# Weights asked for a step sooner, empty rows written in three parts, and first row numbers noted ahead of the scales, in an expert layer

## The reference

```python
x = conv_attention(x)      # group norm, 1x1 qkv, softmax attention, 1x1 out, + normed x
t = to_tokens(x)           # 4 x 1024 tokens of 256
t = t + attention(layernorm(t))          # three residual MLPs, softmax over axis 1, Wout
y = layernorm(layernorm(t)) # with gain and bias the second time
p = softmax(y @ gate_w); keep = top2(p)
out = sum over experts e of keep[:, e] * (gelu(y @ w1[e] + b1[e]) @ w2[e] + b2[e])
t = t + layernorm(t) + out
```

## Time and profile before

| what | us |
|---|---|
| median of 3 runs (lowest, highest) | 1253.4 (1251.55, 1254.43) |
| the profiled execution | 1251.13 |
| its span in the trace | 1249.4 |
| PE busy | 1150.2 (92%) |
| DVE busy | 815.4 (65%) |
| ACT busy | 572.1 (46%) |
| POOL busy | 255.2 (20%) |
| first to last turn mark of the weighted steps, X(2) to X(26) | 359.0 for 24 steps |
| X(26) to X(36) | 116.6 for 10 steps, none with new weights |

### The profile page before, as it was taken

How to read it: one execution, slowest core, us unless ns; L and a number is a source line. 1 busy time by engine, 2 the same in 40 slices (tenths; PEclk the granted TensorE clock), 3 DMA queues, 4 the chain that set the end, 5 groups by cost and what they waited for, 6 DMA issues and landing times.

```text
span 1249.4 us, 24976 instructions
## 1 busy us (share of the span) xinstructions
PE 1150.2 (92%) x8066; PEld 1068.1 (85%) x8067; DVE 815.4 (65%) x1931; ACT 572.1 (46%) x1042; POOL 255.2 (20%) x307
## 2 busy tenths in 40 slices
PE   6999999999999999999999879869789888899993
PEld 5898998988988989989888869869789888899983
DVE  4676476765666855767646777866777788756641
ACT  2433344432536333444324556645556556534431
POOL 2010001000401001411005122344223222323320
PEclk9999999999999999999999989979899999999996
DMA  5001000100101100101003352676674676433238
GB/s 165 1 1 34 1 1 1 35 34 1 63 12 35 34 1 14 59 1 34 1 1 135 99 166 55 187 208 183 193 218 128 182 214 200 116 55 61 57 52 274
DMA packets 82436, 103.50 MB, mean 83 GB/s; under 512 B 11952, under 2 KB 71600, under 8 KB 82352
## 3 DMA queue, kind: packets, MB, share of 16 engines
q1 hardware_dynamic: 68912, 85.10, 21.3%
q0 software_dynamic: 13440, 17.32, 7.4%
HBM read 74.19 MB, written 29.25 MB: 83 GB/s over the span
## 4 chain that ended last, share of the span: by engine, by line
PE 67%; DMA 10%; issue 7%; DVE 6%; SPq 4%; ACT 2%; POOL 2%; POOLq 1%; another core or an unknown queue 0%; ACTq 0%; DVEq 0%
PE ps L1659 59%; DMA w1r<-in_w 4%; DMA acc_rows<-y_w,now_s 4%; PE ps L1753 2%; PE ps L1672 1%; SPq L539 1%; PE ps L1701 1%; DVE w1s L1524 1%; DMA rows<-acc_rows 1%; DVE hs L1622 1%; PE ps L1924 1%; DVE hs L1624 1%; PE ps L1762 1%; PE ps L1775 1%; DVE tl_bn L1144 1%
## 5 line engine op out<-in xcount | busy, mean ns | idle before, releaser
L1659 PE MATMUL ps<-w2s,hs 128*128 128x256 f32 x1728 | 258.1, 285 | 53.0 <-DVE hs L1624 52.8
L1659 PEld LDWEIGHTS ps<-w2s,hs 128*128 128x128 f32 x1728 | 227.0, 193 | 61.3 <-DVE hs L1624 50.4
L1659 PE MATMUL ps<-xt,w1s 128*128 128x256 f32 x1746 | 260.4, 286 | 1.0 <-issue 1.0
L1659 PEld LDWEIGHTS ps<-xt,w1s 128*128 128x128 f32 x1746 | 229.3, 192 | 1.8 <-issue 1.6
L1013 ACT ACTIVATE h<-ps,b1t 128x256 f32<-128x256 f32 x288 | 137.5, 478 | 103.6 <-PE ps L1659 60.0
L750 POOL DMA_INDIRECT acc_rows<-y_w,now_s x72 | 120.3, 1670 | 185.7 <-ACT y_w L1031 120.2
L1624 DVE TENSOR_TENSOR hs<-h,hs 128x256 fp32r<-128x256 f32 x288 | 123.6, 429 | 9.9
L1622 DVE CAST hs<-h 128x256 fp32r<-128x256 f32 x288 | 89.1, 309 | 58.3 <-ACT h L1013 33.9
L1659 PE MATMUL ps<-xs,wh 128*128 128x512 f32 x384 | 121.4, 397 | 1.4 <-issue 1.4
L1659 PEld LDWEIGHTS ps<-vk,pr 128*128 128x128 f32 x768 | 95.8, 190 | 5.1 <-DVE pr L1478 3.0
L1659 PE MATMUL ps<-vk,pr 128*128 128x256 f32 x768 | 97.2, 282 | 2.1 <-DVE pr L1478 2.1
(11 more groups left out here) (232 smaller groups left out, 1779.1 us busy)
## 6 DMA issues: line engine op xcount, KB each, us to landing
w1r<-in_w SPq DMA_DIRECT2D x22, 1024.0 KB
w2r<-in_w SPq DMA_DIRECT2D x22, 1024.0 KB, 8.4
xg<-sorted_rows SPq DMA_DIRECT2D x38, 272.0 KB
b2t<-in_b SPq DMA_DIRECT2D x37, 128.0 KB
xn<-in_x SPq DMA_DIRECT2D x4, 1024.0 KB, 4.8
acc_rows<-r_out SPq DMA_DIRECT2D x4, 1024.0 KB
rows<-acc_rows SPq DMA_DIRECT2D x8, 512.0 KB, 7.7
out_tokens<-cols_out SPq DMA_DIRECT2D x8, 512.0 KB, 8.6
```

The costliest lines, as they stand in the source:

```text
L1659: ins = t.matmul(out, left[l], right[r], start=first and n == 0, stop=last and n == 2, **more)
```

## The change

1. SP's order in turn s becomes `load_weights(s+2)`, `gather(s+2)`, `load_biases(s+1)`, and turn 0 has the weights too. `load_weights(s+2)` waits until the weights of step s are split, where `load_weights(s+1)` waited for those of step s - 1.
2. `write_pads` is cut in three: two blocks at turn 6, three at 7, four at 9.
3. POOL notes steps 0 and 1 before the two `tail_scales`. For this `now_s` and `now_w` get a place of their own.
4. One more pair (steps 10 and 11) is written out, since turn 10 now loads weights of step 12. The waits for the second table (`tab_b`) move along with it.
5. In step 0 PE turns the next rows in chunk 2 and no longer in chunk 1.

```diff
-    LOOP_AT = A_STEPS // 2 - 1
+    LOOP_AT = A_STEPS // 2
...
+        PADS_AT = {6: (0, 1), 7: (2, 3, 4), 9: (5, 6, 7, 8)}
+        ROWS_OUT_AT = 8
...
             def steps(i):                                   # SP
                 for n in range(2):
                     s = i * 2 + n
-                    begin = isinstance(i, int) and s == 0
-                    if not begin:
-                        load_weights(s + 1, 1 - n, (i if n == 0 else i + 1))
+                    unrolled = isinstance(i, int)
+                    if unrolled and s == A_STEPS - 2:
+                        sp.wait_ge(tab_b, 1)
+                    load_weights(s + 2, n, i + 1)
+                    if unrolled and s == A_STEPS - 2:
+                        sp.wait_ge(pad_in, (E + 1) * 16)
+                        sp.wait_ge(rows_in, B * NT * 2 * 16)
                     gather(s + 2, n, False)
-                    if not begin:
+                    if not (unrolled and s == 0):
                         load_biases(s + 1, 1 - n)
-                    if isinstance(i, int):
-                        if s == 6:
-                            write_pads()
-                        if s == 8:
+                    if unrolled:
+                        if s in PADS_AT:
+                            write_pads(PADS_AT[s])
+                        if s == ROWS_OUT_AT:
                             rows_of(B - 1)
...
-            sp.wait_ge(pad_in, (E + 1) * 16)
-            sp.wait_ge(rows_in, B * NT * 2 * 16)
...
-                    note_step(s + 1, 1 - n, (i if n == 0 else i + 1))
+                    if not (isinstance(i, int) and s == 0):
+                        note_step(s + 1, 1 - n, (i if n == 0 else i + 1))
...
+            pool.wait_ge(tab_a, 1)
+            note_step(0, 0, 0)
+            note_step(1, 1, 0)
             tail_scales(B - 1, 0)
             tail_scales(B - 1, 1)
...
-            pool.wait_ge(tab_a, 1)
-            note_step(0, 0, 0)
             pool.wait_ge(tok_out, B * 16)
...
-                    if f == 1:
+                    if f == (2 if isinstance(i, int) and s == 0 else 1):
                         x_turn(s + 1, 1 - n, (i if n == 0 else i + 1))
```

More of the change, by code:

```diff
@@ L144, in hybrid_block_kernel @@
         last_step = sb("last_step", [P, 1], I32)
-        sb("to_512", [P, 0x10])
+        now_s = sb("now_s", [P, 2, SUB], I32)
+        now_f = sb("now_f", [P, 2 * SUB + 1])
+        now_w = now_f[:, 0:2 * SUB].rearrange("p (n h) -> p n h", n=2)
+        limit = now_f[:, 2 * SUB:2 * SUB + 1]
         batch_scope = ExitStack()
@@ L252, in hybrid_block_kernel @@
         y_b = es("y_b", [P, SUB, C])
-        now_s = es("now_s", [P, 2, SUB], I32)
-        now_w = es("now_w", [P, 2, SUB])
+        es("past_y", [P, 16])
         es("past_prob", [P, 512 - 16 + 64])
@@ L569, in steps, with write_pads @@
                     s = i * 2 + n
-                    begin = isinstance(i, int) and s == 0
-                    if not begin:
-                        load_weights(s + 1, 1 - n, (i if n == 0 else i + 1))
+                    unrolled = isinstance(i, int)
[5 more added lines that the diff above has]
+                        sp.wait_ge(rows_in, B * NT * 2 * 16)
                     gather(s + 2, n, False)
-                    if not begin:
+                    if not (unrolled and s == 0):
                         load_biases(s + 1, 1 - n)
-                    if isinstance(i, int):
-                        if s == 6:
-                            write_pads()
-                        if s == 8:
+                    if unrolled:
+                        if s in PADS_AT:
+                            write_pads(PADS_AT[s])
+                        if s == ROWS_OUT_AT:
                             rows_of(B - 1)
-            def write_pads():
+            def write_pads(experts):
                 sp.wait_ge(tab_b, 1)
                 sp.wait_ge(pad_made, 2)
-                for e in range(E + 1):
+                for e in experts:
                     at_row = sp.value_load(pad_at[0:1, e:e + 1], min_val=0, max_val=PAD - STEP) if e < E else PAD
@@ L768, in _ @@
             g.memset(pad_row[:, NUMBER:NUMBER + 1], float(SKIP)).then_inc(pad_made, 1)
-            pool.wait_ge(tab_a, 1)
-            note_step(0, 0, 0)
             pool.wait_ge(tok_out, B * 16)
             for i in range(LOOP_AT):
+                if i == LOOP_AT - 1:
+                    pool.wait_ge(tab_b, 1)
                 steps(i)
-            pool.wait_ge(tab_b, 1)
             pool.wait_ge(tok_out, (B + 1) * 16)
@@ L1636, in _ @@
             for i in range(LOOP_AT):
+                if i == LOOP_AT - 1:
+                    dve.wait_ge(tab_b, 1)
                 steps(i)
-            dve.wait_ge(tab_b, 1)
             with dve.Fori(LOOP_AT, PAIRS) as i:
```

## The result

The changed kernel took **1209.2 us** (median of four runs, 1206.3 to 1212.2) against 1252.5 us for the one before on the same chip: ratio 0.9653, 95% interval 0.9622 to 0.9684, 43 us less. Forecast were 1212.4 us in a range of 1200 to 1235. The profiled run took 1207.3 us, its span 1205.6, at a clock of 0.991.

What follows compares the result with a forecast made beforehand. The prediction took PE's products (59% of the chain) as the bound wherever PE is fed, with waits for weights above that floor. 1251.1 - 7.6 - 14 - 19.4 = 1210.1, plus 2.3 gives 1212.4 us; range 1200 to 1235.

Steps and rivals of the forecast that it cites:

- Step 1: Early notes and weights ahead of the gather remove DVE's whole wait in step 1: -7.6 us, bounds 5.0 and 9.8.
- Steps 7 to 10: Weights ahead of the empty rows end the 14.26 us wait; POOL's rounds are late next: -14 us, between 9 and 24.7.
- Steps 11 to 14 and 16 to 24: The 13 steps with new weights take 12.6 us each, 163.8 for 183.2: -19.4 us, between -31.6 and -4.5.
- a loop of two steps: In weighted steps: splits done, weights issued and landed, rows and biases, gelu, splits; 24.7 us, or 12.35 a step.
- DVE's own 11.7 a step: In the weighted steps, DVE's pieces and a chunk of splits alone would take 11.0 + 0.7 = 11.7 us.
- A: Biases queue behind weights; with landings of 11.8 us weighted steps take 13.75 to 14.0, the whole 1230 us; chance 0.15.
- C: Late biases or rows make PE stand and its clock fall in weighted steps, 16.0 us each: 1263 us; chance 0.05.
- D: Weights don't go out sooner, since splits end hardly before the note; empty rows and notes alone help: 1240 us; chance 0.05.
- B: Landings shrink, all weighted steps reach PE's floor of 11.66 us, steps 7 to 10 win 20: 1194 us; chance 0.10.
- At nothing: Terms of zero: the written-out pair, moved table waits, places of now_s and now_w, steps 2 to 6, 15, 25 to 35.
- What would show it: Signs: ACT's w1r wait under 15 us, step 1 about 14, step 7 below 16, 13 weighted steps at 12 to 13.

Runs made afterwards that it cites:

- experiment 6: The changed kernel with DVE's low parts made half as wide from step 2 on, the other half stale: 1201.6 us, ratio 0.9583.
- experiment 1: The changed kernel with only the weights a step sooner, all nine blocks of empty rows at turn 6, first notes behind the tail scales: 1206.2 us, ratio 0.9612.
- 4: The changed kernel with the first two notes behind the tail scales again: 1207.0 us, ratio 0.9617.
- experiments 5 to 12: Eight follow-up kernels with edits to weight bytes, DVE's work, SP's order, empty rows or row scatters against the changed kernel: medians 1201.6 to 1213.0 us.
- number 12: The changed kernel with only the row scatters spread over steps 5 to 9 as 1, 2, 2, 2, 1 tiles: 1209.9 us, ratio 0.9673.
- 5: The changed kernel with half the bytes in each transfer of weights from step 2 on, so products use stale weights: 1204.1 us, ratio 0.9615.
- 7: The changed kernel with w2 asked for last, behind rows and biases, so only 1 MB lies ahead of the biases: 1212.6 us, ratio 0.9688.
- 11: The changed kernel with empty rows all at turn 6, notes behind the scales, biases before the gather and row scatters spread: 1205.9 us, ratio 0.9632.
- experiments 1 to 4: Four follow-up kernels that take parts of the change back, against the changed kernel: medians 1206.2 to 1242.3 us.
- 9: The changed kernel with SP issuing the biases of the step ahead before the gather: 1205.8 us, ratio 0.9648.
- 10: The changed kernel with empty rows all at turn 6, notes behind the scales and biases before the gather: 1206.8 us, ratio 0.9648.

## Why the prediction was right

**Step 1: right in size, half right in cause.** -7.65 against -7.6. DVE was what is late next, as the prediction put it: it is busy 15.65 of the 15.9 us, and with its low parts half as wide (experiment 6) step 1 takes 14.2. But the wait did not go because of the notes: experiments 1 and 4 have steps 0 and 1 as short with the notes where they were. That the gather no longer stands ahead of the weights is enough; the prediction gave both reasons and took them for one.

**Steps 7 to 10: right in size, and by luck in part.** Forecast were POOL's notes 7 to 10 in 46 us and 11 from there to X(12). The notes after:

```profile
816.92 0.37 POOL L747 CAST now_s<-xg 128x2 int32<-128x2 f32 x1 [6.51 <-DMA acc_rows<-y_w,now_s]
...
832.53 0.21 POOL L747 CAST now_s<-xg 128x2 int32<-128x2 f32 x1 [3.01 <-DMA acc_rows<-y_w,now_s]
...
847.79 0.32 POOL L747 CAST now_s<-xg 128x2 int32<-128x2 f32 x1 [5.57 <-DMA acc_rows<-y_w,now_s]
...
860.93 0.24 POOL L747 CAST now_s<-xg 128x2 int32<-128x2 f32 x1 [3.48 <-DMA acc_rows<-y_w,now_s]
```

15.6, 15.3 and 13.1 us, 44.0 in all (53.5 in the earlier trace rows's run), and 13.3 from there to X(12); since X(8) now lies 1.3 us ahead of note 7, the gain is 9.5 + 4.5 - 1.3 = 12.7. POOL's rounds came as worked out. But the prediction has gelus wait behind these notes, and in this profile they hardly do: the chain over steps 7 to 10 has no piece of POOL in it, and a fifth of it is `issue` (the view cuts the line off):

```profile
by line: PE ps L1670 32.3%; issue 20.5%; DMA b2t<-in_b 9.4%; another core or an unknown queue 4.5%; DVE w1s L1534 4.5%; DVE hs L1632 4.3%; DVE w2s L1534 3.0%; SPq L519 2.9%; DVEq L1605 2.7%; DVE hs L1634 2.5%; ACT w2s L962 2.1%; SPq L552 1.
```

ACT stands 14.4 us there with nothing named that it waits for, and 3.9 for `b2t`, which waited in SP's queue behind weights that stood for DVE's splits. In experiments 5 to 12, where ACT has no such stands, the mechanism of the prediction shows: landings of the token scatters are 24 to 66% of the chain over these steps (40% in number 12), part of which depends on where the window ends. So the rounds hold this stretch in the runs beside it, and in the profiled run of the change another delay of about the same length stood in their place. That less work on POOL would shorten the stretch is not shown: no run takes any away.

**Steps 11 to 14 and 16 to 24: the size was near, the step of the argument was wrong.** 158.7 us against 163.8, 12.2 a step against 12.6. The prediction closed a loop of two steps over the landing of the weights and the biases behind them and got 24.7 us for it (its 1.5 us for 400 KB at 251 GB/s is 1.6). That two steps took 24.3 is luck: no gelu of the loop waits for biases. Experiments 5 and 7 halve what lies ahead of the biases and leave the pace as it is; experiment 6 eases DVE alone and the pace falls to the floor in eight of nine steps. The term that should have been taken was the one that it named and put aside: DVE's own 11.7 a step (11.60 measured), and in place of the 0.25 for short waits the 1.1 us that each end of a pair costs, half of it a step: 11.62 + 0.55 = 12.17. What exactly happens at the end of a pair (the loop's branch, the two low parts that follow the last chunk, or the first gelu that waits for PE's product) was not separated; that less work on DVE removes it is shown. In the ninth step, 16, late biases cost 3.0 us, by POOL's note and not by weights ahead of them. ACT's waits for `b2t` came to 8.2 us, 3 of them, none in the loop.

**The rivals.** A would have shown in over 25 us of waits for `b2t`: 8.2. C wanted the clock below 0.95 from step 16 on: it is 1.00. D wanted ACT's waits for `w1r`: none is left. B was nearest: the loop lies 0.55 us a step above its floor, and the whole at 1209, between its 1194 and the forecast.

**At nothing**: steps 2 to 6 cost 1.0 us more, since one gelu waits for biases that are issued behind the early weights; step 15 costs 0.8 us more, for which no cause was followed up. The gelu:

```profile
813.24 0.47 ACT L1023 ACTIVATE h<-ps,b1t 128x256 f32<-128x256 f32 x1 [3.45 <-DMA b2t<-in_b]
```

**What would show it**: step 7 was to fall below 16 us and took 17.3 (11.6 to 13.2 in experiments 5 to 12); step 1 was to take about 14 and took 16.0, with step 0 shorter by what it is longer: in experiment 1 the two take 15.8 and 14.1 us, and PE waits 1.98 us for `xg` at X(2), which here it doesn't.

## What to carry to other kernels

Put the transfer with the most slack and the longest landing ahead of those that wait for something in the same queue; here that order is worth 48 us in experiment 1, and 30 us where notes and pads had taken their part already; the finer edits around it add nothing that can be told. Where several loops have about the same length, taking one wait away only shows the next: after a gain, measure each part by itself before keeping it, and ease the supposed bound by half before trusting a sum in which it wins by 5%. A chain that runs through three engines and a queue is better tested by the term that is cheapest to halve; an edit that only moves an engine's work to a later step (11 and 12) tests nothing. And where a stretch is compared between profiles, take one of the same chip: the waits for `b2t` of four steps were 3.9 us in the changed kernel and 20.7 in number 12, which has the same order in SP's queue.

## What the runs showed of the hardware that was not expected

In step 7 of the changed kernel ACT, DVE, PE and SP's queue stand at the same time with nothing waited for. ACT between 820 and 832 us:

```profile
826.74 0.47 ACT L1023 ACTIVATE h<-ps,b1t 128x256 f32<-128x256 f32 x1 [4.96 <-remote]
829.75 0.47 ACT L1023 ACTIVATE h<-ps,b1t 128x256 f32<-128x256 f32 x1 [2.02 <-issue]
```

and DVE:

```profile
827.25 0.29 DVE L1632 CAST hs<-h 128x256 fp32r<-128x256 f32 x1 [3.63 <-issue]
```

The clock is 0.90 over this step. It happens again in steps 8 and 9 (2.67 and 4.74 us on ACT). The three long ones stand before a step's seventh or eighth gelu, so they are no waits for biases; the 2.02 us stand before a first gelu and may be one. Such waits are in the steps that are written out (the kernel before had one of 4.0 us on ACT), not in the loop's steps 16 to 24. They go by the set of runs and not by the edit: in steps 7 to 10 ACT's sum is 4.0 to 14.4 us in all six profiles of the kernel before, the change and experiments 1 to 4, and nothing in all eight of 5 to 12, which ran on two other chips than 1 to 4, with nearly the same code. The DMA view has the instruction queues at work there, from 822 to 832 us (packets, MB, share of 16 engines):

```profile
q8 instruction: 1, 0.02, 0.6%
q14 instruction: 1, 0.01, 0.3%
```

Late instructions may be the cause; but kernels 5, 9, 10 and 12 fetch in steps 7 to 10 just what the change does (3 and 4 packets) and have no stall, so the packets alone don't make it, and no run separated it from the chip: it stays open. The Trainium skill, "Runtime: NRT & Kernel Launch", section "Instruction fetch mechanics", says that each engine fetches its instructions in blocks by DMA while it runs and that crossing a block is "mostly hidden"; no run here shows whether these stalls are that.

Without them nothing is won: where the stalls are missing, the gelus wait for `b2t` longer (12.8 to 23.8 us in the four steps of experiments 5 to 12, 3.9 in the change), and the four steps take 58.0 to 64.5 us against 58.6.

Half the bytes of the weights left the DMA engines' share in steps 7 to 10 at 0.71 against 0.82 with all of them, at 195 GB/s in place of 240: the rows, pads and scatters, which the edit doesn't touch, keep the engines busy, and bytes alone say little of it.

```profile
814.60:872.80 58.20, 50.58 (x402) 49.78 (x401) 41.53 (x96) 34.94 (x77) 30.98 (x30) 0.94 0.71 195
```
